# A fused attention and feed-forward kernel: feed-forward weight codes kept in DRAM, and projections and transpositions in another order

## What is computed

```python
x = x + tanh(g_xattn[0]) * mha(layernorm(x), ctx, ctx, W_Q, b_Q, ..., W_O, b_O)      # 16 heads of 32
x = x + tanh(g_ffn[0])   * bitnet_ffn(layernorm(x), w_gate, w_up, w_down)             # inner size 2048
x = x + tanh(g_xattn[1]) * plain_attention(layernorm(x), ctx)
x = x + tanh(g_ffn[1])   * mxfp4_linear(x, weight, bias, delta_w, delta_act)

def _weight_quant(w):                       # for w_gate, w_up and w_down
    scale = 1.0 / clip(mean(abs(w)), 1e-5)
    return clip(round(w * scale), -1, 1) / scale
```

## Time and profile before

| | |
|---|---|
| median of 3 runs | 1636.88 us (1634.34 to 1637.41) |
| the profiled execution | 1635.9 us, its span 1634.1 us |
| busy, share of the span | PE 90%, DVE 76%, POOL 56%, ACT 54% |
| granted TensorE clock, mean | 0.948 |
| last product of the attention part | 877.2 us |
| first product of the feed-forward | 894.3 us |

### The profile page before, as it was taken

One profiled execution on the slowest core, in us unless ns is written; L12 is line 12 of the kernel. 1 busy time (PEld: TensorE's weight loads), 2 busy tenths in 40 slices (PEclk: granted clock), 3 DMA queues, 4 the chain that ended last, 5 costly groups with the idle time before them and its releaser, 6 DMA issues. The chain is left out here.

```text
span 1634.1 us, 24705 instructions
## 1 busy us (share of the span) xinstructions
PE 1475.7 (90%) x6969; PEld 932.6 (57%) x6969; DVE 1241.7 (76%) x2141; ACT 874.5 (54%) x1434; POOL 918.9 (56%) x1160
## 2 busy tenths in 40 slices
PE   5699999899998999999674899999999978999997
PEld 4466556566565656566321455555555546877785
DVE  3567787877879767767664688888888858998996
ACT  4265556565555565555543455555555545655552
POOL 3166676585675676665555343433344326778775
PEclk9899999999999999999765999999999999999998
DMA  5836749375583846648765244444444564556531
GB/s 174 252 111 195 225 149 269 99 230 170 162 245 121 260 138 194 186 123 242 197 181 154 72 114 109 106 108 109 115 108 110 150 189 132 165 159 202 168 87 62
DMA packets 247020, 259.03 MB, mean 159 GB/s; under 512 B 140028, under 2 KB 156936, under 8 KB 243208
## 3 DMA queue, kind: packets, MB, share of 16 engines
q1 hardware_dynamic: 246920, 257.85, 55.4%
HBM read 149.50 MB, written 76.58 MB: 138 GB/s over the span
## 5 line engine op out<-in xcount | busy, mean ns | idle before, releaser
L704 ACT ACTIVATE a_probs<-a_sc 128x512 f32<-128x512 f32 x512 | 300.2, 595 | 295.4 <-PE a_sc L600 294.2
L789 DVE TENSOR_REDUCE a_negmax<-a_mx 128x1 f32<-128x512 f32 x512 | 337.6, 674 | 94.6 <-PE a_mx L583 93.6
L914 POOL TENSOR_TENSOR a_acc<-a_acc,a_probs 128x512 f32<-128x512 f32 x256 | 330.7, 1323 | 21.5 <-ACT a_probs L704 20.8
L914 POOL TENSOR_TENSOR a_acc<-a_probs 128x512 f32<-128x512 f32 x128 | 166.3, 1318 | 256.8 <-ACT a_probs L704 255.9
L583 PE MATMUL a_mx<-a_stack 96*128 96x512 f32 x512 | 230.6, 450 | 52.3 <-DVE a_negmax L789 40.4
L600 PE MATMUL a_sc<-a_stack 97*128 97x512 f32 x512 | 218.6, 429 | 24.9 <-ACT a_probs L704 18.0
L1065 PE MATMUL bank<-wcode,b_xq 128*128 128x512 bf16 x1024 | 228.1, 381 | 7.8 <-DMA b_xq<-b_xcode 7.8
L1065 PEld LDWEIGHTS bank<-wcode,b_xq 128*128 128x128 bf16 x1024 | 100.3, 98 | 130.9 <-DMA b_xq<-b_xcode 9.7
L583 PEld LDWEIGHTS a_mx<-a_stack 96*128 96x128 f32 x512 | 101.1, 198 | 128.6 <-DVE a_negmax L789 78.9
L795 DVE RECIPROCAL a_attn<-a_den 128x128 f32<-128x128 f32 x128 | 120.9, 948 | 59.8 <-PE a_den L628 59.8
L1103 ACT ACTIVATE b_sig<-bank,b_tok 128x512 f32<-128x512 f32 x128 | 87.6, 684 | 90.6 <-PE bank L1065 88.5
(11 more groups left out here) (165 smaller groups left out, 2646.7 us busy)
## 6 DMA issues: line engine op xcount, KB each, us to landing
a_stack<-spill SPq DMA_DIRECT2D x192, 256.0 KB, 4.8
spill<-k_part SPq DMA_DIRECT2D x64, 512.0 KB, 3.5
ctx_t<-k_wo SPq DMA_DIRECT2D x16, 1024.0 KB, 8.1
c_ct<-ctx_t SPq DMA_DIRECT2D x8, 2048.0 KB, 8.5
a_stage<-in_x_dram SPq DMA_DIRECT2D x32, 256.0 KB, 5.0
a_stage<-in_ctx_dram SPq DMA_DIRECT2D x32, 256.0 KB, 2.7
attn_t<-a_attn SPq DMA_DIRECT2D x32, 256.0 KB, 4.4
b_xin<-in_x_dram SPq DMA_DIRECT2D x32, 256.0 KB, 2.7
```

The costliest lines, as they stand in the source:

```text
L704: nc.scalar.activation(probs[:, k, j, :], sc[i % 2][:], ACT.Exp, scale=SCALE).then_inc(exp_done, 1)
L789: nc.vector.tensor_reduce(negmax[:, g % 2, j, t:t + 1], mx[i % 2][:], axis=AX.X, op=ALU.max, negate=True).then_inc(mx_done, 1)
L914: nc.gpsimd.tensor_tensor(acc[:, j], probs[:, 0, j] if k == 1 else acc[:, j], probs[:, k, j], ALU.add)\
```

## The change

**Codes.** The matrices are taken in 12 units of a MB. Each is loaded and summed in one group (1 to 12, counted over all batches), in the burst. From group 14 to 28 (with the group 1 of each batch left out) each is loaded again into the one buffer `wsum`, rounded by ACT (two halves), clipped by DVE (two halves, in place, and then all of it) in the burst, and stored to DRAM (`code_t`). In the last batch the codes are transposed by DMA from DRAM, four in each of groups 0 to 2. W_O is split in the burst of group 1 of the last batch. The rounding of `weight` moves to the start: all four parts, spread over the first 20 maxima of batch 0; some of its operations work on all 2048 numbers at once.

**Last group.** The very last group has no additions on POOL: PE sums `probs` itself (`add_up`, 16 products into `den`), and its `pv` products are spread between the scores.

**Order.** x is transposed one group earlier, between V steps; then come Q of groups 0 and 1 with ctx transpositions between them, then K of group 0, and the rest evenly. `RANK` numbers the eight projections in the new order.

**Join.** JOIN goes from 3190 to 3165.

```diff
+    UNITS = 3 * CH
...
+    SUM_FIRST, QSTEPS = 1, 6 + 6 * C
+    CODE_IN = {n: k for k, n in enumerate((14, 15, 16, 18, 19, 20, 22, 23, 24, 26, 27, 28))}
...
-        tx_at, tc_at = (0, 1.5, 3, 4.5), (10.8, 12.3, 13.8, 15.3)
-        qk_at = {(0, Q): 6, (0, K): 16.8, (1, Q): 21.4, (1, K): 26, (2, Q): 30.6, (2, K): 35.2, (3, Q): 39.8, (3, K): 44.4}
+        tx_at, tc_at = (-14, -12.4, -6.5, -5), (4.2, 6.2, 9, 12.8)
+        v_at = (0, 0.85, 1.7, 2.55, 4, 4.85, 5.7, 6.55, 7.4, 8.25, 9.1, 9.95, 11.5, 12.35, 13.2, 14.05)
+        qk_at = {(0, Q): (0, 1.2, 2.4, 3.6), (1, Q): (7.2, 8.3, 9.4, 10.5)}
+        qk_at.update({key: [14.3 + 5.2 * n + 1.3 * c for c in range(C)] for n, key in enumerate(((0, K), (1, K), (2, Q), (2, K), (3, Q), (3, K)))})
...
-                    ck.add(ahead(qk_at[g, side] + 1.15 * c), 3, "qk", g, side, c)
-                ck.add(ahead(qk_at[g, side] + 1.15 * (C - 1)) + at["spill"], 9, "spill", g, side)
+                    ck.add(ahead(qk_at[g, side][c]), 3, "qk", g, side, c)
+                ck.add(ahead(qk_at[g, side][C - 1]) + at["spill"], 9, "spill", g, side)
                 ck.add(ahead(fill_at[g, side]), 9, "fill", g, side)
...
-            ck.add(base + 20, 9, "sload", g)
-            ck.add(base + BURST + 2, 9, "sum", g)
-        ck.add(BURST + at["den"], 9, "wscale")
-        ck.add(-60, 9, "wload1")
-        for n in range(QSTEPS):
-            ck.add(PERIOD * (n // 6) + BURST + n % 6, 9, "wquant", n)
-        ck.add(2 * PERIOD + 30, 9, "wstore1")
-        for k, tick in enumerate(ITEM_AT):
...
-            ck.add(tick + 40, 9, "rclip", k)
-            ck.add(tick + 44, 9, "rcode", k)
-            ck.add(tick + 50, 9, "rturn", k)
-        ck.add(3 * PERIOD + 30, 9, "boload")
-        ck.add(4 * PERIOD - 10, 9, "boscale")
+            ck.add(base + BURST + 26, 9, "uload", g + 1, "sum")
+            if g != 1:
+                ck.add(base + (-36 if g == 2 else 38), 9, "uload", g, "code")
+            ck.add(base + BURST + 2, 9, "sum", g, 0)
+            ck.add(base + BURST + 10, 9, "sum", g, 1)
+            ck.add(base + BURST + 2, 9, "uround", g, 0)
+            ck.add(base + BURST + 10, 9, "uround", g, 1)
+            ck.add(base + BURST + 12, 9, "uclip", g, 0)
+            ck.add(base + BURST + 20, 9, "uclip", g, 1)
+            ck.add(base + BURST + 29, 9, "ucode", g)
+            ck.add(base + BURST + 44, 9, "ustore", g)
+            if g < T - 1:
+                for n, tick in enumerate((5, 35, 65, 100)):
+                    ck.add(base + tick, 9, "uturn", g, n)
+        ck.add(PERIOD + BURST + at["den"], 9, "wscale")
+        ck.add(PERIOD + 60, 9, "woload")
...
+        for k, tick in enumerate((74, 88, 112, BURST + 14)):
+            ck.add((G - 1) * PERIOD + tick, 6, "pv_last", G - 1, k)
...
+                    elif name == "ustore" and b * G + args[0] in CODE_IN:
+                        k = CODE_IN[b * G + args[0]]
+                        sp.wait_ge(u_code, k + 1)
+                        sp.dma_start(code_t[k].rearrange("p (a n) -> p a n", a=4), codes).then_inc(u_stored, 16)
+                    elif name == "uturn" and b == NB - 1:
+                        k = args[0] * CH + args[1]
+                        sp.wait_ge(u_stored, 16 * (k + 1))
                         if k == 0:
                             sp.wait_ge(qk_full, 2 * G * NB)
...
+                        if k == 2 * CH:
                             sp.wait_ge(v_full, T * NB)
-                        sp.dma_start_transpose(wcode[:, n * CH + c], codes[:, CODE_SLOT[k], :]).then_inc(r_turned[CODE_SLOT[k]], 16)
+                        sp.dma_start_transpose(wcode[:, k], code_t[k]).then_inc(gu_turned if k < 2 * CH else down_turned, 16)
...
+                def add_up(k):
+
+                    for j in range(J):
+                        last = nc.tensor.matmul(den[DH * j:DH * (j + 1), :], ones[:], probs[:, k, j, :], start=k == 0, stop=k == T - 1)
+                    return last
...
+                        slot_n = g * T * J + i - 1
+                        if it + shift == 0 and 0 <= slot_n < 5 * C:
+                            if slot_n % 5 == 0:
+                                quantise(6 + slot_n // 5 * 6)
+                            quantise(6 + slot_n // 5 * 6 + 1 + slot_n % 5)
...
+                    elif name == "uclip" and (it + shift) * G + args[0] in CODE_IN:
+                        g, h = args
+                        k = CODE_IN[(it + shift) * G + g]
+                        half = slice(h * 1024, (h + 1) * 1024)
+                        dve.wait_ge(u_round, 2 * k + h + 1)
+                        if h:
+                            dve.wait_ge(u_clip, 2 * k + 1)
+                        nc.vector.tensor_scalar(codes[:, 2 * h:2 * h + 2], wsum[:, half].rearrange("p (a n) -> p a n", a=2), ROUND, 1.0, ALU.subtract, ALU.min).then_inc(u_clip, 1)
+                    elif name == "ucode" and (it + shift) * G + args[0] in CODE_IN:
+                        k = CODE_IN[(it + shift) * G + args[0]]
+                        dve.wait_ge(u_clip, 2 * k + 2)
+                        nc.vector.tensor_scalar(codes, codes, -1.0, None, ALU.max).then_inc(u_code, 1)
...
-    JOIN, SCALE = 3190, 0.64
+    JOIN, SCALE = 3165, 0.64
```

315 lines of the change are left out of this document (150 added, 165 removed).

## The result

The changed kernel takes 1625.25 us (median of 5 runs, 1621.99 to 1626.58) against 1636.09 (5 runs, 1634.02 to 1637.41): 0.9935 times as long, with a 95% interval of 0.9924 to 0.9945. It is faster, by 10.8 us, where 50 were forecast, and the time lies above the range. The profiled execution is the one of 1625.25 us, with a span of 1623.5.

What follows compares the result with a forecast made beforehand. PE was taken as the bound in V groups, with waits and clock costing some 50 of the middle's 659 us. Terms -35 -2 -8 -12 -8 +3 +12 = -50 took 1636.9 to 1587 us, range 1560 to 1612.

Steps and rivals of the forecast that it cites:

- Last batch, -35: Last batch's four groups: codes mostly moved out and the last group without POOL additions, 86.1 us against 121.3.
- End, -2: End of the attention: last reciprocals no longer start behind a clip, 2 us saved.
- x transpositions, -8 and -12: Middle: transposing x among V steps removes waits for `xt` (-8), and even spacing regains time lost to the clock (-12).
- The bound that I gave groups 1 to 3, POOL at 23 us: Groups without V steps: POOL's twelve additions need 15.2 us after a 7.8 us start, so 23.0 us a group.
- a forecast of 641: Middle stretch, 657.2 us before, was forecast to become 16 us shorter.
- Rounding of `weight`, -8 and +3: Moving it out of bursts of batches 1 to 4 saves 8 us; the start, where it goes, costs 3.
- Sums, 0: ACT's two sums a group in 12 groups are covered by the burst, so they cost nothing.
- Codes, +12: Twelve coded bursts: DVE's clips end at or behind the burst's end, delaying reciprocals, 1 us each.
- The second and fourth rivals: Second: DVE late after coded bursts, middle gains nothing, 1608 us (0.23). Fourth: clips and additions lock each other, 1679 us (0.04).
- the queue is otherwise idle there: SP's queue: loads and stores wait for steps a burst earlier, so transpositions and loads were given no cost.
- The bound of 10 us: Upper bound for DRAM transpositions in the last batch, if they delay the `mrow` transfer each group's first score needs.
- Third rival: Last batch: DRAM transpositions take over 10 us each, outlast three groups by 50 us; 1637 us, no change (0.04).

Runs made afterwards that it cites:

- e14: e8 with only one DRAM transposition in the first group of the last batch and two x transpositions 0.4 and 0.45 slots later: 1587.4 us.
- e16: e14 with the last group's denominator and `pv` products set one by one between scores instead of in lumps: 1589.7 us.
- e8: e7 with the three fills of K of group 2 moved from ahead of `mrow` to the start of the next group's slots: 1596.1 us.
- e20: Kernel before with the new order, the store of the last K behind `mrow` and the fills of K of group 2 later: 1620.6 us.
- e1: Changed kernel with the old tables of positions, and steps 3 to 5 of the rounding of `weight` at K of group 0: 1625.5 us.
- e2: Kernel before with the new tables of positions and nothing else, the new order alone: 1638.8 us.
- e3: Changed kernel with one store, K of group 3, moved from right ahead of the `mrow` transfer to behind it: 1617.5 us.
- e7: e3 with the last DRAM transposition of each last-batch group behind `mrow`, and group 3's unit load behind the fills of group 1's K: 1608.0 us.

## Why the prediction was wrong

The forecast was 50 us and 10.8 were measured. Of the difference, 21.7 us lie in the middle, 9.4 in the last batch, 5.1 in the start and 3.2 in the feed-forward part.

- **Last batch, -35: -25.2 measured** (121.3 to 96.1 us). Group by group 25.5, 29.3, 22.0 and 19.3 against 24.5, 23.3, 23.8 and 14.5. The first two hold late transfers (waits of 1.8 and 7.5 us); without them they take 23.5 and 22.2 us in e14, and the third took 22.0: these three were forecast 1 to 2 us too long. The last group was mis-sized by 4.8 us. I let the `pv` products and denominators hide between the scores. They stand in lumps, between two scores of PE: 3.6 us the first, at a granted clock of 0.50, 2.1 the next. ACT runs dry behind each:

```profile
857.82 1.08 ACT L727 ACTIVATE a_probs<-a_sc 128x512 f32<-128x512 f32 x2 [3.12 <-PE a_sc L611]
860.74 1.78 ACT L727 ACTIVATE a_probs<-a_sc 128x512 f32<-128x512 f32 x3 [1.84 <-PE a_sc L611]
864.20 0.60 ACT L727 ACTIVATE a_probs<-a_sc 128x512 f32<-128x512 f32 x1 [1.68 <-PE a_sc L611]
```

The lumps are a part of it: with them split, e16's last group still takes 17.7 us.

- **End, -2: right.** The first feed-forward product waits 13.7 us, 16.1 before.
- **x transpositions, -8 and -12: the gain is there, but covered up.** The waits for `xt` went; 9.5 us for V's eviction (in the V group, now 27.2 us instead of 23.5) and 10.4 for `part` and the ctx tiles of DVE (in group 1), which I didn't count, came in their place. The clock is 0.98 in the changed kernel, and 1.00 in e8. The order with the queue mended takes 15.8 us off the middle (e20), where I had 20.
- **The bound that I gave groups 1 to 3, POOL at 23 us, was 1.3 us too high.** Groups 2 and 3 of batches without codes take 21.6 to 21.8 us, and `den` starts 0.05 to 0.08 us after POOL's last addition, so POOL is the bound. But the first addition starts 6.5 us after the product's start, not 7.8, and twelve take 15.0 to 15.2. I had read the 7.8 off a V group.
- **The middle of e8, 640.1, against a forecast of 641, is in part luck.** The order is worth less than forecast (15.8, not 20), codes and rounding together cost nothing there (e8 is 1.3 us below e20, where +4 was forecast), and the gain at the fills of K wasn't counted.
- **Rounding of `weight`, -8 and +3: right in the old order.** In e1 the groups that stood behind the rounding in batches 1 to 4 take 23.4, 23.6, 23.9 and 23.6 us, before 25.2, 25.0, 26.9 and 25.7, which is 8.3 us. In the new order it is some 2. Its start is 1.8 us later. The start of the changed kernel is 8.1 us later: the first score is at 79.64 instead of 75.13, and the first group takes 27.1 us instead of 23.6. What I left out is the new order in batch 0. The x transpositions are in the first V group (27.0 us in e20, 28.1 in e2). And the first product of maxima starts at 50.7 us, 48.2 in e2, 44.5 in e1 and 45.9 before; this part of the delay was not taken apart.
- **Sums, 0: right.** Groups 2 and 3 of batches 1 and 2 take 21.8 and 21.6 us, without a wait at the bursts.
- **Codes, +12: near the measured size, for the wrong reason.** The middle of the changed kernel is 12.2 us longer than e2's, which has the rounding of `weight` instead of the codes. I put it on DVE. The three clips do end late, 0.6 to 1.0 us after the denominators' product in most bursts, and one of 1024 numbers takes from 0.69 to 2.69 us (24 of them, median 0.95). Each of the twelve that take over 1 us began while an addition of POOL ran, and ended 0.55 us after an addition ended. That agrees with the Trainium skill (SBUF — State Buffer, section SBUF: two separate sides) and the exclusive lock that it describes. One reading of the prediction was wrong: POOL adds beside the clips of the last batch too. There a clip starts at the end of one addition and the next addition is the one that waits: it takes 1.8 to 2.0 us, where 1.3 is usual. But in e8, with the same clips, a coded group 3 takes 22.1 us where an uncoded one takes 21.65. The second and fourth rivals, which built on it, fall with it.
- **The step that failed** is half a sentence on the transpositions and loads: "the queue is otherwise idle there". It is not, and delays of what stands behind them were put at nothing in the middle. From 455 to 475 us the DMA engines are as full before the change (share 0.99 to 1.08) as after (0.80 to 1.07). I had costed the steps of the new order on PE and DVE alone. I hadn't written down which stores and fills move with them past `mrow`, nor what a megabyte per unit does to those behind it. The bound of 10 us "where they delay the `mrow` transfer" named the mechanism and gave it one place of three. The waits are 19.6 us (10.3 in the middle and 9.3 in the last batch) for `mrow` and 7.1 with "issue". e8 brings back 29 us by moving nothing but transfers, 22.8 in the middle and 5.2 in the last batch by its profile; e14 brings a further 9, with one more such move and two x transpositions of PE.
- **Third rival** (transpositions outlast the groups): they land in 5.6 us in the median, 4.3 from SBUF, and don't outlast anything. Two of the twelve landed after 10.0 and 10.4 us, which I had named as a sign of being wrong. They did harm by what stood behind them.

Left open are the join, the 1 to 2 us by which starts differ from run to run, and the kernel before with only the queue moves, which wasn't run.

## What to carry to other kernels

When a step moves, write out the issuing queue around it and add up bytes: what stands ahead of a small transfer that an engine waits for, divided by the GB/s that the windows show, is how long it takes to land; count what hasn't landed yet, here from the time when the queue was last empty. Here one store (7.7 us, e3) and three fills (12.0, e8 against e7), moved by a few ticks, were worth more than the whole change (10.8). A better order of work can read as no gain at all while another resource is late, so judge it with that resource mended, and in the batches where the extra work is. And look into every row of waits before a change, also one that names no engine.

## What was not expected of the hardware

In the changed kernel an 8 KB transfer took between 1.8 and 9.6 us to land, by what was issued ahead of it. A DMA transposition out of DRAM kept SP's queue for 2.0 to 7.3 us, so that a transfer behind it wasn't even issued. And waits of 1 to 4 us cost more than themselves: at 471.12 the wait is 3.8 us, but that group is 5.9 us longer than the V group a batch earlier, whose wait was 0.2 (33.6 against 27.7); products at half the clock follow it (0.50 from 470 to 475 us).
